# 20 of the first sort's 32 blocks scattered to DRAM by GpSimd

## The reference, cut to what matters

```python
edge_index = jnp.stack([src, dst])
xn = _layernorm(x, axis=-1)
x = x + _L0_gnn_ref(xn, ...) + _L0_mix_ref(xn[None], ...)[0]
x = x + _L0_ffn_ref(_layernorm(x, axis=-1)[None], ..., L0_ffn_edge_index)[0]
# in _L0_ffn_ref:
e = leaky_relu(a_src[src] + a_dst[dst], 0.2)
e_max = segment_max(e, dst); ee = exp(e - e_max[dst]); denom = segment_sum(ee, dst)
agg = segment_sum(h[src] * (ee / denom[dst])[:, :, None], dst)
```

## Time and profile before

| what | us |
|---|---|
| time before, median of 3 runs | 4229.22 (4228.53 to 4237.3) |
| the profiled execution's own time | 4231.31 |
| its span | 4229.6 |
| first sort, from its first load to the barrier | 6 to 416 |
| move pass inside it | 236 to 407 |
| first mix stage | 416 to 574 |
| attention | 574 to 837 |
| second norm | 837 to 883 |
| edge stage: gathers, and the expert work beside them | 883 to 1630 |
| rest of the edge stage up to the second sort | 1630 to 1924 |

### The profile page before, as it was taken

How to read it: one execution, slowest core, us unless ns; L and a number is a source line. 1 busy time by engine, 2 the same in 40 slices (tenths; PEclk the granted TensorE clock), 3 DMA queues, 4 the chain that set the end, 5 groups by cost and what they waited for, 6 DMA issues and landing times. The chain is left out here.

```text
span 4229.6 us, 46886 instructions
## 1 busy us (share of the span) xinstructions
PE 2316.3 (55%) x15074; PEld 1750.8 (41%) x15074; DVE 1804.4 (43%) x3989; ACT 1390.4 (33%) x3199; POOL 1305.0 (31%) x1271
## 2 busy tenths in 40 slices
PE   3876826441111016994762055544453656989888
PEld 3632425330011004663632044433342444688887
DVE  8898559810000000226896843443343466011112
ACT  2588357410000001222591012434343522133332
POOL 0000410047777771000002027453535221522221
PEclk8999967755555557996995576677676676999999
DMA  2300240031101110011222133342434220433534
GB/s 64 119 15 12 54 87 1 1 63 21 13 8 12 12 12 22 31 35 65 100 61 71 39 89 85 121 150 92 158 103 139 103 72 22 128 125 125 182 127 105
DMA packets 166124, 300.75 MB, mean 71 GB/s; under 512 B 77078, under 2 KB 128137, under 8 KB 158580
## 3 DMA queue, kind: packets, MB, share of 16 engines
q1 hardware_dynamic: 103592, 167.52, 13.1%
q0 software_dynamic: 62400, 131.73, 11.1%
HBM read 265.96 MB, written 105.32 MB: 88 GB/s over the span
## 5 line engine op out<-in xcount | busy, mean ns | idle before, releaser
L1792 POOL DMA_INDIRECT ge_near<-gat_src,s_other x512 | 520.8, 1017 | 166.7 <-issue 166.7
L2114 PE MATMUL bank<-arena 128*125 128x256 f32 x800 | 218.3, 436 | 629.3 <-issue 591.3
L2967 POOL DMA_INDIRECT he_buf<-wh_dram,s_other x400 | 385.6, 964 | 413.2 <-DVEq L3201 290.9
L2114 PEld LDWEIGHTS bank<-arena 128*125 128x125 f32 x800 | 169.6, 217 | 685.1 <-issue 633.2
L2146 DVE TENSOR_TENSOR XN<-bank,arena 125x256 f32<-125x256 f32 (+1 forms) x100 | 42.4, 425 | 954.5 <-DMA g_al<-al_dram,g_idx 712.9
L2127 ACT ACTIVATE arena<-bank,arena 128x500 f32<-128x500 f32 (+1 forms) x112 | 69.9, 633 | 933.3 <-DMA s_a_dram<-XN 548.3
L2647 ACT ACTIVATE x_hT<-bank,x_w 128x128 f32<-128x128 f32 x448 | 164.5, 367 | 337.4 <-PE bank L2591 310.4
L2591 PE MATMUL bank<-x_xT,x_w 128*128 128x128 f32 x1792 | 234.1, 295 | 47.5 <-DMA x_w<-in_L_ffn_packed,x_rows 47.5
L2591 PEld LDWEIGHTS bank<-x_xT,x_w 128*128 128x128 f32 x1792 | 231.5, 210 | 54.8 <-issue 52.7
L3087 ACT ACTIVATE he_buf<-he_buf,he_e 128x128 f32<-128x128 f32 x800 | 239.4, 387 | 37.3 <-issue 34.9
L1529 POOL IOTA gj_node<- 128x125 f32 x1 | 0.2, 239 | 674.3 <-POOLq L73 674.3
(11 more groups left out here) (720 smaller groups left out, 5894.6 us busy)
## 6 DMA issues: line engine op xcount, KB each, us to landing
he_result<-he_buf SPq DMA_DIRECT2D x25, 2080.0 KB
XN<-s_a_dram SPq DMA_DIRECT2D x57, 512.0 KB
x_y<-XN SPq DMA_DIRECT2D x24, 448.0 KB
ge_near<-gat_src,s_other POOLq DMA_INDIRECT x512
x_x<-zero SPq DMA_DIRECT2D x1, 7196.0 KB, 40.3
x_xs<-x_x SPq DMA_DIRECT2D x56, 128.5 KB
he_buf<-wh_dram,s_other POOLq DMA_INDIRECT x400
arena<-x_y SPq DMA_DIRECT2D x2, 2800.0 KB
```

The lines of the kernel that those rows point to most:

```text
L1792: pool.indirect_dma_start(out=G[:, c, 0:HF + H], out_offset=None, in_=m.gat_src, in_offset=bass.IndirectOffsetOnAxis(ap=ed.other[:, c:c + ...
L2114: last = pe.matmul(m.ps[4 + j % 2][:P, 0:D], self.hT[:, f, j * P:(j + 1) * P], w.w2[e][:, f, :], start=f == 0, stop=f == FC - 1)
L2967: pool.indirect_dma_start(out=buf[j][:, c, 0:HF + H], out_offset=None, in_=m.wh_dram, in_offset=bass.IndirectOffsetOnAxis(ap=ed.other[:, t ...
```

## The change

GpSimd takes 20 of the move pass's 32 blocks, which are 320 of the 512 columns. For each column it issues one indirect DMA that writes the 128 values (4 bytes each) to their places in a DRAM table, then clears an unused 80-column piece of a tile and waits for its own pipeline (`drain`). The 320 sends are spread over four stages by count: 48 after the ranks of the first three blocks, 56 after those of block 20, 32 ahead of the gathers of `mix0_start` and 6 behind them, 156 in `mix0_attention`, 22 in the norm. In that norm's stage SyncE loads the table once all have landed, and VectorE adds it to what the matmuls have moved. SyncE clears the table with one DMA ahead of the sort's loads. VectorE, ScalarE and TensorE run 12 blocks in the move pass in place of 32. VectorE has one operation more in the sort's setup, which writes the values for GpSimd, and two at the end of the norm.

```diff
+class Placing:
+    BLOCKS = 20
+    def clear(self, sp):
+        zeros = self.m.zero16[:, 0:512].bitcast(FP32)
+        self.cleared(sp, self.rows().rearrange("p (a b) -> p a b", b=256),
+                     zeros.unsqueeze(1).broadcast_to((128, self.ed.cols // 256, 256)))
+    def learn(self, pool, pos, blocks):
+        lo, hi = self.known * BC, blocks * BC
+        pool.wait_ge(self.ranked, blocks)
+        pool.tensor_copy(self.goal[:, lo:hi], pos[:, lo:hi])
+        pool.drain()
+        self.known = blocks
+    def send(self, pool, n):
+        for c in range(self.begun, self.begun + n):
+            pool.indirect_dma_start(out=self.table, out_offset=bass.IndirectOffsetOnAxis(ap=self.goal[:, c:c + 1], axis=0),
+                                    in_=self.val[:, c:c + 1], in_offset=None).then_inc(self.sent[c % 2], 16)
+            pool.memset(self.rest, 0.0)
+            pool.drain()
+        self.begun += n
+    def load(self, sp, back):
+        for i in range(2):
+            sp.wait_ge(self.sent[i], 16 * (self.total // 2))
+        self.loaded(sp, back, self.rows())
+    def add(self, dve, back):
+        dve.wait_ge(self.loaded.sem, 16)
+        dve.tensor_tensor(back, self.moved[:, :], back, ALU.add)
+        dve.drain()
+        dve.tensor_scalar(self.ed.other[:, :], back, Sort.MID, None, ALU.add).then_inc(self.added, 1)
...
 # mix0_start, gpsimd
+            placing.send(pool, 32)
             pool.wait_ge(nodes.w_ready, 1)
             pool.wait_ge(nodes.stored.sem, nodes.stored.all)
             edges.gather(pool)
+            placing.send(pool, 6)
...
 # mix0_attention, gpsimd
             pool.memset(pw[:, :, :], 0.0).then_inc(zeroed, 1)
+            placing.send(pool, 156)
...
 # Sort.vector: the move pass over nm = nb - 20 blocks
-        tiles(dve, self.nb, 4, lambda t, j: self.vector_move(dve, t, j))
+        tiles(dve, self.nm, 4, lambda t, j: self.vector_move(dve, t, j))
...
 # Sort.vector_setup
+            dve.tensor_scalar(p.val[:, :], ed.other[:, 0:p.total], float(N - 1), -self.MID, ALU.min, ALU.add).then_inc(p.valued, 1)
...
 # Sort.scalar
-        tiles(act, self.nb, 4, lambda t, j: self.scalar_move(act, t, t, self.nr))
+        tiles(act, self.nm, 4, lambda t, j: self.scalar_move(act, t, t + self.off, self.nr))
...
 # sort_edges
             def _(sp):
+                placing.clear(sp)
                 s.sync(sp, lambda sp: x_loaded.nodes(sp, m.X[:, :].rearrange("p (t d) -> p t d", d=D),
                                                      m.io["x"].rearrange("(t p) d -> p t d", p=P)))
                 sp.wait_ge(x_loaded.sem, x_loaded.all)
...
+            @block.gpsimd
+            def _(pool):
+                placing.first(pool)
+                for t in range(3):
+                    placing.learn(pool, s.pos, t + 1)
+                    placing.send(pool, BC)
+                placing.learn(pool, s.pos, placing.BLOCKS)
+                placing.send(pool, 56)
...
 # GatNodes.store, after the third of five stores
+            if t == 10:
+                self.placing.load(sp, self.back[:, :])
...
+    def beside(self, pool, normed):
+        self.placing.send(pool, self.placing.total - self.placing.begun)
+    def after(self, dve):
+        self.placing.add(dve, self.back[:, :])
```

More of the change, by code:

```diff
@@ L544, with mix0_start @@
 OC = 6
-def mix0_start(m):
+def mix0_start(m, placing):
     nc, io = m.nc, m.io
@@ L689, in log_exp_scale, with mix0_attention @@
     dve.drain()
-def mix0_attention(m, routes):
+def mix0_attention(m, routes, placing):
     nc, io = m.nc, m.io
@@ L936, in __init__, with rows, first @@
         self.start = m.dram(tag + "_start", [KEYS + 1], I32)
+class Placing:
+    BLOCKS = 20
+    def __init__(self, m, ed, room):
+        self.m, self.ed = m, ed
+        self.total = self.BLOCKS * BC
+        self.goal, self.val = room.other[:, 0:self.total], room.key[:, 0:self.total]
+        self.moved = ed.other[:, :].bitcast(FP32)
+        self.rest = room.key[:, self.total:]
+        self.table = m.dram("pl_table", [128 * ed.cols, 1])
+        self.cleared, self.loaded = Loads(m, "pl_cleared"), Loads(m, "pl_loaded")
+        self.sent = [m.sem(f"pl_sent{i}") for i in range(2)]
+        self.ranked, self.valued, self.added = m.sem("pl_ranked"), m.sem("pl_valued"), m.sem("pl_added")
+        self.begun = self.known = 0
+    def rows(self):
+        return self.table.rearrange("(p c) one -> p (c one)", p=128)
+    def clear(self, sp):
+        zeros = self.m.zero16[:, 0:512].bitcast(FP32)
+        self.cleared(sp, self.rows().rearrange("p (a b) -> p a b", b=256),
+                     zeros.unsqueeze(1).broadcast_to((128, self.ed.cols // 256, 256)))
+    def first(self, pool):
+        pool.wait_ge(self.valued, 1)
+        pool.wait_ge(self.cleared.sem, self.cleared.all)
+    def learn(self, pool, pos, blocks):
[5 more added lines that the diff above has]
+    def send(self, pool, n):
+        assert self.begun + n <= self.known * BC
+        for c in range(self.begun, self.begun + n):
[13 more added lines that the diff above has]
+        dve.tensor_scalar(self.ed.other[:, :], back, Sort.MID, None, ALU.add).then_inc(self.added, 1)
 def floor_div(dve, q, r, pos, cols):
@@ L990, with __init__ @@
     SPLIT = 3221225472.0
-    def __init__(self, m, ed, key_in, other_in, line_in, sb, H):
+    def __init__(self, m, ed, key_in, other_in, line_in, sb, H, placing=None):
+        self.placing, self.off = placing, 0 if placing is None else placing.BLOCKS
         self.m, self.ed, self.key_in, self.other_in, self.line_in = m, ed, key_in, other_in, line_in
@@ L995, in __init__ @@
         self.cols, self.nb = cols, cols // BC
+        self.nm = self.nb - self.off
         self.ki = sb(tag + "_ki", [128, cols], I32)
@@ L1028, in __init__ @@
         self.q, self.r = self.tmp[:, 0:cols], self.tmp[:, cols:2 * cols]
-        self.nr = self.pos
+        self.nr = self.pos if placing is None else sb(tag + "_nr", [128, cols])[:, :]
         self.q2, self.r2 = self.a2, self.b2
@@ L1119, in vector_setup @@
         dve.tensor_scalar(self.val2[:, :, :], twice(ed.other[:, :]), float(N - 1), -self.MID, ALU.min, ALU.add)
+        if self.placing is not None:
+            p = self.placing
+            dve.tensor_scalar(p.val[:, :], ed.other[:, 0:p.total], float(N - 1), -self.MID, ALU.min, ALU.add).then_inc(p.valued, 1)
         dve.drain()
@@ L1168, in vector_choose @@
         dve.drain()
-        dve.tensor_reduce(self.pos[:, at(t, BC)], self.pick[:, :, :], AX.X, ALU.add)
+        done = dve.tensor_reduce(self.pos[:, at(t, BC)], self.pick[:, :, :], AX.X, ALU.add)
+        if self.placing is not None:
+            done.then_inc(self.placing.ranked, 1)
         dve.drain()
@@ L1186, in vector_move @@
         oav = self.wide(self.oav[j % 2])
+        u = t + self.off
         dve.wait_ge(self.used4, t * 2 + 2)
-        dve.tensor_tensor(oav, self.pairs(self.q2[:, at(t, BC), :], BC, 128), self.row(BC, 128), ALU.is_equal)
+        dve.tensor_tensor(oav, self.pairs(self.q2[:, at(u, BC), :], BC, 128), self.row(BC, 128), ALU.is_equal)
         dve.drain()
-        dve.tensor_tensor(oav, oav, self.pairs(self.val2[:, at(t, BC), :], BC, 128), ALU.mult)
+        dve.tensor_tensor(oav, oav, self.pairs(self.val2[:, at(u, BC), :], BC, 128), ALU.mult)
         for h in range(2):
             dve.tensor_tensor(self.wide(self.rv[2 * (j % 2) + h]),
-                              self.pairs(self.r2[:, bass.ds(t * BC + 8 * h, 4), :], 4, self.cols),
+                              self.pairs(self.r2[:, bass.ds(u * BC + 8 * h, 4), :], 4, self.cols),
                               self.row(4, self.cols), ALU.is_equal).then_inc(self.hot4, 1)
     def vector_move_start(self, dve, t):
-        j = self.nb + t
+        j = self.nm + t
         dve.wait_ge(self.used4, 2 * j + 2)
@@ L1207, in vector_finish @@
         m, ed, cols = self.m, self.ed, self.cols
-        moved, marks = 2 * self.nb + 4, 2 * self.nb + 8
+        marks = 2 * self.nm + 8
         diff, sums = self.q, self.r
@@ L1219, in vector_finish @@
         dve.drain()
-        dve.tensor_scalar(ed.other[:, :], diff, self.MID, None, ALU.add)
+        if self.placing is None:
+            dve.tensor_scalar(ed.other[:, :], diff, self.MID, None, ALU.add)
+        else:
+            dve.tensor_copy(self.placing.moved[:, :], diff)
         dve.tensor_tensor_scan(ed.key[:, :], m.ones[:, 0:cols], m.ps[0][:, 0:cols], 0.0, ALU.mult, ALU.add)
@@ L1251, in tensor @@
             self.tensor_rank(pe, nb - 1, g, nb - 1)
-        for near, far, blocks, first in ((m.ps[6], m.ps[7], nb, 0), (m.ps[0], m.ps[1], 2, nb)):
+        for near, far, blocks, first in ((m.ps[6], m.ps[7], self.nm, 0), (m.ps[0], m.ps[1], 2, self.nm)):
             near, far = near[:, 0:self.cols], far[:, 0:self.cols]
@@ L1344, in scalar_move, with sort_edges @@
             last.then_inc(self.far4, 1)
-def sort_edges(m, ed, key_in, other_in, line_in):
+def sort_edges(m, ed, key_in, other_in, line_in, placing):
```

(13 more changed lines are left out.)

4 lines of the change are left out of this document (2 added, 2 removed).

## The result

The changed kernel takes 4601.63 us (4596.51 to 4604.66, 4 runs) against 4228.88 us: a ratio of 1.0886, 95% interval 1.085 to 1.0922. That is 373 us slower, where 4147 was forecast and 4250 was the top of the range.

What follows compares the result with a forecast made beforehand. ScalarE was taken to pace the move pass, VectorE 0.1 us behind, in a chain of barriers. -98.4 + 1.0 + 0.3 + 4.3 + 2 + 6 + 3 = -81.8 gave 4149.5, as median 4147 us; range 4120 to 4250.

Steps and rivals of the forecast that it cites:

- The saving: Move pass: 20 of 32 blocks go from its engines, 20 x 4.92 = 98.4 us less; bounds 96 to 99.
- clear, values and tail: Added work: SyncE's clearing DMA 1.0 us, VectorE's values for GpSimd 0.3, the norm's table load and add 3.
- The neighbours' price: VectorE operations beside sends lengthen 0.07 us each: rank pass 4.3, first mix stage 2, attention 6; in sum 12.3.
- The fourth rival: Each send locks out VectorE's two-port operations, 0.265 us per operation: +36 us, 4182; chance 0.04.
- The sends: GpSimd's 320 sends (DMA, memset, drain): a period of 1.7 us, range 1.33 to 5.7, with nothing exposed at 1.7.
- the first rival: The drain waits for the send to land: period 4 to 5.7 us, at 5.3 a time of 5250; chance 0.16.
- the break-even of 2.08: The send period, in us, at which the sends' overshoot equals the saving of 82 us.
- The overshoot sum: Sends times period less the room in sort, mix stage, attention and norm; 1104 us at a period of 5.3.
- The third rival: GpSimd's unbroken DMAs stretch other engines' turns in the sort to 11.2 us per block: +110, 4257 us; chance 0.07.

Runs made afterwards that it cites:

- bare sends: The changed kernel with neither memset nor drain behind each send; 3183.9 us on a chip B (kernel before 3275.9), 4480.4 on a chip A (before 4232.3).

## Why the prediction was wrong

- **The saving** was right in sum: 98.4 forecast, less 4.3 for clear, values and tail, is 94.1; the edge stage starts 94.1 earlier without sends. The close match is partly luck: the sort saved 95.1 where these terms give 97.1, and the tail cost about 1 where 3 was allowed.
- **The neighbours' price** was too high, on the safe side: 12.3 forecast on three engines. With sends unbroken on B it is 3.8, against a run without sends on A; a run without sends on B was not made. Under the drain the attention's own work took 262 us, as before. The fourth rival, a lock of 0.265 us per VectorE operation, did not appear: L1134 kept its mean (748 ns before, 747 after), and L683 and L684 went from 168 to 220 and from 160 to 207.
- **It was GpSimd that was held**, which no term priced. Its DMA takes 0.96 us alone and 0.96 to 0.97 (means) beside the rank pass's reductions and the attention's reciprocals; beside the move pass's `tensor_tensor` it took 1.4 to 2.0, beside L1134 1.2 to 1.5, and up to 2.9 in the attention. The Trainium skill, page SBUF — State Buffer, section Who interferes with whom, says that VectorE's two-port operations, `tensor_scalar` among them, starve the building of descriptors. It says that `tensor_tensor` with both inputs in SBUF contends only with GpSimd's reads, and that it was not seen to stall a DMA. The trace agrees for L1134, a `tensor_scalar`; for `tensor_tensor` it differs, with some 0.7 us per send in the move pass, and the measurement decides. Whether the send's reading of its 128 places is what was held stays open.
- **The step that failed is "The sends": "I take 1.7".** It is 2.9 alone, 3.3 in the sort, 3.28 in the attention. The mechanism is that of the first rival, which had a chance of 0.16: the drain waits for the landing. I set it aside because "a drain is for the engine's pipeline"; the runs show that it covers the engine's own DMAs, since it ends 0.07 us behind their landing. The argument that an operation ran 0.07 after a scatter proved nothing on the drain behind it. The other argument was misread: the DMA engines were three quarters busy before that wait, not in it (0.97 from 3600 to 3620, but 0.24 from 3632 to 3641).
- **The first rival's price was wrong too**, 5.3 where it is 2.9 to 3.3. The kernel before had half of the number, in the profile's list of DMA issues (last figure: us from issue to landing), for the scatters of rows 6:

```profile
x_x<-XN,x_slot POOLq DMA_INDIRECT x50, 3.8
```

  There the next scatter started 6.11 us after the one ahead of the drain (3641.38 - 3635.27), and 3.8 of these were landing, so 2.3 lay outside it. I used the 4.53 whole and hardly asked how the landing would shrink with rows of 4 bytes. Even with a landing of nothing these rows leave 2.3, past the break-even of 2.08. They would thus have told the sign, but not the size: the landing is 2.2, and the part outside it 0.8. One reason is that the old drain stood behind a row of unbroken scatters. It ended 1.2 us after the last landing that the trace has; the one drain of the changed kernel behind unbroken gathers ended 1.6 after its send's. What it waits for there stays open.
- **The overshoot sum** was right once the periods are put in: at the measured 3.3 / 3.28 / 3.1, 104 x 3.3 - 204 = 139 (141 measured), a gather start 50 later (49), 156 x 3.28 - 266 = 246 (250), 22 x 3.1 - 41 = 27 (31).
- **The third rival** (unbroken DMAs stretch the others' turns) played no part in the result, because the drain breaks the row, but it holds on A once the drain is gone: the sort then lost 131 us, where it had 110. I had given it a chance of 0.07, and read rows 10 as a wait on a transfer.

## What to carry to other kernels

A `drain` behind a GpSimd DMA is a wait for its landing: price it as issue to landing plus the restart, at the landing that the traffic of that stretch allows, and ask what a counted number of sends then needs against each window. Two sends on their way, tied by their semaphores, brought the mean period down to between 1.6 and 1.8. That fitted the windows here but for the attention, which took 271.0 us, against 265.7 with bare sends; it was tried only on chips B, where unbroken DMAs are harmless. Before GpSimd's DMAs are put beside other work, look in the trace at hand for what the others do beside an unbroken row of them: in the same 64 us of the sort TensorE was busy 19 us on a chip A and 54 on a chip B.

## What had not been expected of the hardware

- While GpSimd issues DMAs 0.30 us apart, the other engines of chips A wait up to 22 us in the attention and 31 in the sort to hand over, in one stretch in multiples of 5.6. A memset between DMAs takes back 79 of the 170 us that the attention had lost (353.9 against 433.2), and 2 us of the 131 in the sort; a drain behind every fourth leaves the sort 37 us longer than without sends. On chips B nothing of it shows. The cause was not found: whether it lies in the semaphores, in the instruction streams or in the chips' setting stays open.
- A scatter of 4 bytes for each of 128 rows lands after 2.2 us, and after up to 11.0 beside a 7 MB clear. A `drain` behind it ends 0.07 us later, and the next DMA starts 0.77 us behind the landing.
